# A mixture with soft slots in a Perceiver kernel: one set of logits, turned for the dispatch weights

## What is computed

```python
x_ln = (x - mean) / sqrt(var + LN_EPS) * gamma + beta
x_n, mu_n = _l2norm(x_ln, -1) * scale, _l2norm(mu, 0)
logits = einsum('bnd,des->bnes', x_n, mu_n)
dispatch = softmax(logits, axis=1)                           # over the tokens
combine = softmax(logits.reshape(B, N, E * S), axis=-1)      # over all slots
slot_in = einsum('bnd,bnes->besd', x_ln, dispatch)
h = gelu(einsum('besd,edh->besh', slot_in, W1) + b1)
slot_out = einsum('besh,ehd->besd', h, W2) + b2
out = einsum('bsd,bns->bnd', slot_out.reshape(B, E * S, D), combine)
```

## Time and profile before

| | |
|---|---|
| median of 3 runs | 1651.22 us |
| lowest, highest | 1647.46, 1653.78 us |
| span of the profiled execution, first to last instruction | 1649.2 us |
| time of the profiled execution | the profile gives its span, 1649.2 us, and no time beside it |
| PE busy | 1459.9 us (89% of the span) |
| DVE busy | 1061.0 us (64%) |
| ACT busy | 843.3 us (51%) |
| POOL busy | 424.9 us (26%) |
| mean granted clock of PE | 0.943 of full speed |
| `l1_ffn` | 541 to 628 us of the span |

### The profile page before, as it was taken

The page is one execution under the profiler, slowest core; times in us unless marked ns, Lnnn a source line. Parts: engine busy times, 40 slices in busy tenths (PEclk is TensorE's granted clock), DMA queues, the critical chain, the costliest instruction groups (busy, mean ns, idle before and its releaser), DMA issues. The chain is left out here.

```text
span 1649.2 us, 25002 instructions
## 1 busy us (share of the span) xinstructions
PE 1459.9 (89%) x8552; PEld 1040.0 (63%) x8552; DVE 1061.0 (64%) x2194; ACT 843.3 (51%) x2244; POOL 424.9 (26%) x513
## 2 busy tenths in 40 slices
PE   7877988858997889987799999999999889999969
PEld 5653444436755477776577777787787436666657
DVE  4687989735675566655355655345443579999953
ACT  2447989821123373354334444243343478999931
POOL 2243000000000003412224224224220017777710
PEclk9976999968998899988899999999999999999979
DMA  3003999946421414001000000000000343333120
GB/s 140 1 1 75 179 182 185 183 131 184 127 80 32 96 36 139 1 1 52 1 1 1 1 1 1 1 1 1 1 1 1 122 141 115 116 116 116 40 71 13
DMA packets 190489, 110.85 MB, mean 67 GB/s; under 512 B 150121, under 2 KB 166505, under 8 KB 189468
## 3 DMA queue, kind: packets, MB, share of 16 engines
q1 hardware_dynamic: 190364, 109.26, 25.4%
HBM read 75.41 MB, written 0.26 MB: 46 GB/s over the span
## 5 line engine op out<-in xcount | busy, mean ns | idle before, releaser
L672 DVE TENSOR_REDUCE x_row_max<-banks 128x1 f32<-128x512 f32 x248 | 152.4, 680 | 15.4 <-PE banks L366 15.3
L575 ACT ACTIVATE x_v_full<-banks,x_neg_max,x_q_scale 128x1024 int16<-128x1024 f32 x128 | 153.3, 1201 | 15.8 <-DMA x_v_full<-x_v_full 8.9
L2390 PE MATMUL banks<-x_v,ctx_tokens 128*128 128x128 f32 x1088 | 148.7, 277 | 11.2 <-ACT ctx_tokens L2555 6.2
L212 PE MATMUL banks<-a_w_ring,x_normed_T 128*128 128x512 f32 x320 | 146.6, 598 | 4.8 <-DVE a_r L3162 4.8
L2390 PEld LDWEIGHTS banks<-x_v,ctx_tokens 128*128 128x128 f32 x1088 | 134.0, 192 | 16.0 <-ACT ctx_tokens L2555 7.7
L2638 DVE TENSOR_REDUCE x_small<-banks 128x1 f32<-128x2048 f32 x32 | 73.3, 2291 | 86.8 <-PE banks L2371 86.8
L2371 PE MATMUL banks<-x_kT,ctx_tokens 128*128 128x512 f32 x256 | 118.8, 608 | 4.3 <-ACT x_exps L2537 4.3
L2479 POOL TENSOR_TENSOR ctx_tokens<-ctx_tokens 128x512 f32<-128x512 f32 (+1 forms) x48 | 54.4, 1133 | 232.0 <-DVE ctx_tokens L2620 232.0
L366 PE MATMUL banks<-x_kT_parts,x_qT_int 64*128 64x512 bf16 x512 | 103.5, 408 | 6.5 <-DVE x_row_max L672 3.1
L427 PEld LDWEIGHTS banks<-x_v_full,x_v_int 128*16 128x16 f16 x1024 | 57.7, 91 | 77.8 <-DMA x_v_full<-x_v_full 45.9
L212 PEld LDWEIGHTS banks<-a_w_ring,x_normed_T 128*128 128x128 f32 x320 | 59.1, 192 | 68.8 <-issue 68.8
(11 more groups left out here) (526 smaller groups left out, 3300.2 us busy)
## 6 DMA issues: line engine op xcount, KB each, us to landing
a_w_ring<-in_L_attn_WB_T SPq DMA_DIRECT2D x16, 512.0 KB
a_w_ring<-in_L_attn_WC_T SPq DMA_DIRECT2D x16, 512.0 KB
f_w_gate_up<-in_L_ffn_gate_up SPq DMA_DIRECT2D x18, 352.0 KB
ctx_tokens<-in_ctx SPq DMA_DIRECT2D x16, 256.0 KB, 5.7
a_w_ring<-in_L_attn_Wth_T SPq DMA_DIRECT2D x8, 512.0 KB
a_bias_ring<-in_L_attn_B_bias_perm SPq DMA_DIRECT2D x16, 256.0 KB
a_bias_ring<-in_L_attn_C_bias_perm SPq DMA_DIRECT2D x16, 256.0 KB
f_w_down<-in_L_ffn_down SPq DMA_DIRECT2D x18, 176.0 KB
```

Of the source, the lines that this page charges most:

```text
L212: last = nc.tensor.matmul(out, lhsT, rhs, start=(i == 0), stop=(i == len(pairs) - 1))
L575: nc.scalar.activation(eb[:, q % RING], k.ps[:, 2 + 2 * (q % 2):4 + 2 * (q % 2), :].rearrange("p a n -> p (a n)"), ACT.Exp, bias=nb[:, v % ...
L672: nc.vector.reduce_max(mx[:, u % 2, i:i + 1], k.bank(MBANK[m % 3]), AX.X).then_inc(s.max_taken, 1)
L2390: last = nc.tensor.matmul(k.bank(7, P, HD3), et[:, (n * NG + g) % 2, j % 4], vt[:, u % 2, j], start=(j == 0), stop=(j == KT3 - 1))
```

## The change

The dispatch logits are no longer a product of their own. The combine logits (tokens x slots, already multiplied by the norms) are finished first, and `turn_logits` transposes 128 x 128 blocks of them into bank 0. The pieces are made with both batch rows of the same 512 slots one after the other: pieces 0 to 3 ahead of the loop, 4 and 5 in iteration 0, 6 and 7 in iteration 1; the first products go two by two into iterations 1 and 2. Since `comb` must keep the logits until they are turned, the combine exponentials are written to `cexp`, which lies in the memory of `mu`; DVE gives the first of them free only when all eight pieces are multiplied, and ACT does both in iteration 2. The norm columns (`mu_col`, `ncol`, `mu_ready`) go, with the transposes and the copy that made them.

```diff
@@ l1_attn, PE
-                pe.wait_ge(s.kk_ready, 1)
-                for q4 in range(4):
-                    last = nc.tensor.transpose(k.bank(1, P, P, q4 * P), k.mu_norm[:, q4 * P:(q4 + 1) * P], k.ident[:])
-                last.then_inc(s.col_in_psum, 1)
@@ l1_attn, ACT
-                act.wait_ge(s.col_in_psum, 1)
-                nc.scalar.copy(k.mu_col[:]..., k.bank(1)...).then_inc(k.mu_ready, 1)
@@ l1_ffn
-        ncol = sb("neg_mu_rnorm", [P, ne])
+        cexp = k.mu[:].rearrange("p c s -> p (c s)").rearrange("p (b s) -> p b s", b=B)
@@ PE
                 def combine_logits(n):
-                    b, j = divmod(n, 4)
+                    j, b = divmod(n, B)
+                    if b == 0 and j == 0:
+                        pe.wait_ge(s.xT_ready, B)
...
-                def dispatch_logits(p):
-                    if p == 0:
-                        pe.wait_ge(s.xT_ready, B)
-                    else:
+                def turn_logits(p):
+                    pe.wait_ge(s.logits_taken, B * (p // 2 + 1))
+                    if p >= 1:
                         pe.wait_ge(s.dexp_ready, 4 * p)
                     for e in range(2):
                         a = (2 * p + e) * SLOTS
-                        last = matmul_acc(nc, k.bank(0, P, BT, e * BT), [(k.mu[:, c, a:a + SLOTS], xst[:, c]) for c in range(DC)])
+                        for b in range(B):
+                            last = nc.tensor.transpose(k.bank(0, P, P, (e * B + b) * T), comb[:, b, a:a + SLOTS], k.ident[:])
...
-                steps = ((0, dispatch_logits), (1, turn), (3, turn_combine), (2, hidden), (3, slot_out), (4, combine))
+                for n in range(4):
+                    combine_logits(n)
+                steps = ((0, turn_logits), (1, turn), (3, turn_combine), (2, hidden), (3, slot_out), (4, combine))
...
-                        if lag == 1 and i < 2:
-                            for n in range(4 * i, 4 * i + 4):
+                        if lag == 0 and i < 2:
+                            for n in range(4 + 2 * i, 6 + 2 * i):
                                 combine_logits(n)
-                        if lag == 1 and i == 1:
-                            for n in range(4):
+                        if lag == 1 and i in (1, 2):
+                            for n in range(2 * i - 2, 2 * i):
                                 first_product(n)
@@ ACT
-                act.wait_ge(k.mu_ready, 1)
...
                             nc.scalar.activation(disp[:, r, e, b], k.bank(0, P, T, (e * B + b) * T), ACT.Exp, bias=dm[:, r, 1, e, b:b + 1],
-                                                 scale=k.mu_col[:, 2 * p + e:2 * p + e + 1], accum_out=dm[:, r, 2, e, b:b + 1]).then_inc(s.dexp_ready, 1)
+                                                 accum_out=dm[:, r, 2, e, b:b + 1]).then_inc(s.dexp_ready, 1)
...
-                    nc.scalar.activation(comb[:, b], comb[:, b], ACT.Exp, bias=sm[:, b, 4:5], accum_out=sm[:, b, 5:6]).then_inc(s.cexp_ready, 1)
+                    nc.scalar.activation(cexp[:, b], comb[:, b], ACT.Exp, bias=sm[:, b, 4:5], accum_out=sm[:, b, 5:6]).then_inc(s.cexp_ready, 1)
...
                     if i in (1, 2):
-                        combine_exps(i - 1)
-                    if i == 1:
-                        for n in range(4):
+                        for n in range(2 * i - 2, 2 * i):
                             take_product(n)
+                    if i == 2:
+                        for b in range(B):
+                            combine_exps(b)
@@ DVE
-                dve.wait_ge(k.mu_ready, 1)
-                nc.vector.tensor_scalar(ncol[:], k.mu_col[:], -1.0, None, ALU.mult)
...
                     if j == 3:
                         link(last)
+                        if b == 0:
+                            dve.wait_ge(s.logits_ready, 8)
...
-                    nc.vector.tensor_tensor(dm[:, r, 1], dm[:, r, 0], ncol[:, 2 * p:2 * p + 2].unsqueeze(2).to_broadcast([P, 2, B]), ALU.mult).then_inc(s.dmax_ready, 1)
+                    nc.vector.tensor_scalar(dm[:, r, 1], dm[:, r, 0], -1.0, None, ALU.mult).then_inc(s.dmax_ready, 1)
...
+                for n in range(4):
+                    take_logits(n)
                 for i in range(NPAIR + 3):
...
                     if i < 2:
-                        for n in range(4 * i, 4 * i + 4):
+                        for n in range(4 + 2 * i, 6 + 2 * i):
                             take_logits(n)
```

More of the change, by code:

```diff
@@ L103, in __init__ @@
         self.mu_norm_ready = ctx.enter_context(nc.semaphore("mu_norm_ready"))
-        self.mu_ready = ctx.enter_context(nc.semaphore("mu_ready"))
         self.mask_bias_ready = ctx.enter_context(nc.semaphore("mask_bias_ready"))
@@ L1114, in l1_attn @@
         with signals(nc, k.pool, "dve_step xt_ready proj_ready low_ready exp_ready dec_ready scanned den_in_psum den_ready o_ready out_ready "
-                     "select_ready row_in_psum row_taken col_in_psum kk_ready") as s, nc.Block() as block:
+                     "select_ready row_in_psum row_taken kk_ready") as s, nc.Block() as block:
             @block.sync
@@ L1167, in _ @@
                     nc.scalar.copy(k.mu_row[:, j * 512:(j + 1) * 512], k.bank(ROW_BANK[j])).then_inc(s.row_taken, 1)
-                act.wait_ge(s.col_in_psum, 1)
-                nc.scalar.copy(k.mu_col[:].rearrange("p (j q) -> p q j", j=4), k.bank(1).rearrange("p (q j r) -> p q j r", q=4, j=4)[:, :, :, 0]).then_inc(k.mu_ready, 1)
             @block.gpsimd
@@ L1331, in turn_combine @@
                         for b in range(B):
-                            last = nc.tensor.transpose(k.bank(2, P, P, (e * B + b) * T), comb[:, b, a:a + SLOTS], k.ident[:])
+                            last = nc.tensor.transpose(k.bank(2, P, P, (e * B + b) * T), cexp[:, b, a:a + SLOTS], k.ident[:])
                     last.then_inc(s.ct_in_psum, 1)
@@ L3391, in build @@
                 k.xscale = k.sb("x_scale", [P, 1], F32, to_f1)
-                k.mu_col = k.sb("mu_rnorm_cols", [P, EXPERTS], F32, to_f1)
                 k.musq = k.sb("mu_squares", [P, DC, EXPERTS * SLOTS], F32, to_f1)
```

## The result

| | before | changed |
|---|---|---|
| median of 12 runs each, same chip | 1653.28 us | 1646.11 us |
| lowest, highest | 1647.46, 1659.02 us | 1644.2, 1649.72 us |
| span of the profiled execution | 1649.2 us | 1643.4 us |
| its own time | not given | 1645.1 us |
| `l1_ffn`, first DVE statistics to the end of the last write | 86.41 us | 79.20 us |

The ratio is 0.996, with an interval of 0.9948 to 0.9971: 7.2 us less, 0.43%. By the bound of 0.5% this is "the same", as forecast, and by the interval it is a real gain. The median is 1.2 us above the forecast of 1644.9. That closeness is partly luck: the gain was 0.9 us larger than the forecast 6.3, and the median of before was 2.1 us higher in these runs than in the three that the forecast started from.

What follows compares the result with a forecast made beforehand. The prediction took PE to bound the pair loop, after a head where PE, DVE and ACT wait for one another. Loop 3.6 plus head 2.7 made 6.3 us, from a median of 1651.2 to 1644.9 us; range 1640 to 1650.

Steps and rivals of the forecast that it cites:

- The total: Whole kernel: 3.6 us from the pair loop plus 2.7 us from the stage's head, 6.3 us saved, giving 1644.9 us.
- the chances' likeliest case: Whole kernel: a time within 0.5% (8.3 us) of before, called the same; chance 0.73.
- The head: Stage before exponentials 3: they start at 583.3 instead of 586.03 us, a gain of 2.7 us.
- The walk: Stage before exponentials 3: step-by-step timing of PE, DVE and ACT in the new order, ending with exponentials 3 at 583.3 us.
- ACT becomes the bound: Pair loop: PE's iteration falls from 6.19 to 4.91 us, 0.06 under ACT's 4.97, so ACT sets the period.
- The loop: Exponentials 4 to 7: three periods shorten from 18.48 us together to 4.97 each, saving 3.6 us; period 3 to 4 stays.
- The tail: From exponentials 7 to the stage's last write: nothing changes, since the last dispatch product lies earlier; gain nothing.
- The load: Table load ahead of exponentials 0: with one wait removed it runs during the pieces, 1.30 us less on the path.
- Half clock in the loop: Pair loop: PE's clock falls after its wait and stays down, 9.8 us an iteration; four such give 1664 us; chance 0.06.
- The head gains nothing: Stage before the loop: exponentials 3 start no earlier than 586.0 us, only the loop gains, 1647.6 us; chance 0.15.
- the loop gains nothing: Pair loop: turn, maximum and exponentials close at 6.2 us as before, only the head gains, 1648.5 us; chance 0.08.
- More than 8.3 us: Whole kernel: earlier starts against clock changes and differences between runs bring about 1641 us or less; chance 0.21.

## Why the prediction was right, and where its steps were off

- **The total.** 6.3 us forecast, 7.2 us measured, in the stage and in the medians alike. The direction, the chances' likeliest case and the range hold.
- **The head, 2.7 us.** 44.71 to 41.47 is 3.24. The walk was right: exponentials 0 come 12.1 us after the pieces start (12.2 forecast), exponentials 3 35.0 after (35.5). What it lacked is the cheaper exponential; with the operand put back the head gains 2.72.
- **"ACT becomes the bound" at 4.97 us.** This step failed. 4.97 is right only with the operand; the changed kernel's ACT needs 4.61, and PE's 4.90 is the bound, as in before. Even with the operand put back PE had hardly a gap, since it came late to the loop after the fall of its clock, where the forecast had ACT hold it up. The forecast had the value among its bounds ("if it saved as much as 0.1 us of each 0.45, 0.4 us a pair") and took the other end, by a fixed cost worked out from one instruction of 2048 columns. That instruction has its input elsewhere and none of the operand in question, so it bounded nothing.
- **The loop, 3.6 us.** From exponentials 3 to 7 it was 23.45 us and is 19.48: 3.97. PE's iteration is 4.90 us where 4.91 was worked out. Had the clock held, these four periods would take 18.44 us, as with PE kept busy; the fall took 1.0 of that. So the forecast's 3.6 is near by luck: the cheaper exponential, which it put at nothing, was worth 1.4 us more here (5.0 in place of 3.6), and the fall of the clock, which it put at nothing too, took 1.0 back.
- **The tail, nothing.** 18.25 us before and after.
- **The load, 1.30 us in the head.** Measured 1.34 at exponentials 3, and the drain that the Trainium skill adds ("ScalarE: Activation LUTs", What ACT_TABLE_LOAD costs) was again not there: to make the load wait cost 1.34 us, not 2.66.
- **Half clock in the loop.** The rival came true in small: the wait it named was there (2.20 us, with 1.22 behind it; "about 2.7" forecast), the clock fell, and was full again after PE had worked through 584 to 587. The forecast said that such a short fall hides behind ACT; as PE and not ACT was the bound, it did not, and cost 1.0 us. Four slow iterations, 1664 us, are excluded. Of the Trainium skill's statement that transposes do not count as busy in the same way for the clock ("TensorE: Matmul & The Clock Gate", Part 4: PE-mode transpose): the loop, with 1.3 to 1.4 us of transposes in each 4.9 us, ran at 0.98 over 587.5 to 607 and at 1.00 over 592 to 607; the trace does not show such a loop held back by its transposes.
- **"The head gains nothing" and "the loop gains nothing".** Neither: 3.24 and 3.97.
- **"More than 8.3 us", 0.21.** Not reached by this change; the kernel with one exponential moved reaches it (10.9 us). The forecast took the place of the combine exponentials as given and did not see the 1.7 us of idle ACT beside it.

The order's value is the one cause that the forecast left mixed: it booked 2.7 us to the new head. The order alone, as it stands in the changed kernel, gains nothing there; it pays together with the product that it makes needless, the freed load and the cheaper exponential.

## What to carry to other kernels

When the same numbers are needed in two layouts, making them once and turning them was cheaper than a second product in a loop that PE bounds: 1.72 us became 0.44 here, and the reordering that this forces cost 0.3 us or nothing. When a step is removed from the bound engine, compute the next engine's period with its changed instructions, operand by operand, since 0.09 us an instruction decided whether ACT needed more time a pair than PE, 4.97 us against 4.90, or less, 4.61. Then look for the waits of PE at the edges of its loops: one exponential moved into ACT's idle time, and a few useless products in two of them, brought as much again as the change.

## What was not expected of the hardware

- An activation of 128x128 out of the matmul memory takes 0.46 us with a column of scale factors and 0.37 without; only the bias column remained.
- A wait that is long fulfilled can cost 1.3 us: as the second wait of an activation it pushes the first onto the table load ahead of it, which could otherwise run early.
- Behind two waits of PE, 2.20 and 1.22 us with some 0.6 us of turns between them, the clock was at half, at a price of about 1.0 us. Behind the same two waits in the kernel whose load waits it fell later, at a price of 0.3 us; with the first wait at 1.76 us (logits turned twice) or cut to 0.48 us by useless products it stayed full.
- One execution to the next, the same scan stage took 27.63 and 28.78 us, by the clock, and by a wait for a DMA ahead of its first product, 1.29 us in one and 1.82 in the other. A single run's total says nothing on one microsecond; the length of the changed stage, which two profiles gave within 0.2 us, does.
